# A routed feed-forward stage that gathers its tokens by a slot table and adds into the output rows in place

## The reference

```python
top_w, top_i = jax.lax.top_k(xf @ Wg + bg, 2)
top_w = jax.nn.softmax(top_w, axis=-1)
w_dense = jnp.sum(jax.nn.one_hot(top_i, E) * top_w[..., None], axis=1)
for e in range(E):                       # E = 8, W1 256 x 1024, W2 1024 x 256
    h = jax.nn.gelu(xf @ W1[e] + b1[e], approximate=False)
    out = out + w_dense[:, e:e + 1] * (h @ W2[e] + b2[e])
```

## Time and profile before

| | us |
|---|---|
| median of 3 executions | 6163.82 |
| lowest and highest | 6153.75, 6172.43 |
| the profiled execution | 6173.5 |
| its span, first to last instruction | 6171.7 |
| PE busy | 4328.9 (70%) |
| DVE busy | 3208.3 (52%) |
| ACT busy | 2796.2 (45%) |
| POOL busy | 3500.6 (57%) |

### The profile page before, as it was taken

One profiled execution on the slowest core, in us unless ns is written; L12 is line 12 of the kernel. 1 busy time (PEld: TensorE's weight loads), 2 busy tenths in 40 slices (PEclk: granted clock), 3 DMA queues, 4 the chain that ended last, 5 costly groups with the idle time before them and its releaser, 6 DMA issues. The chain is left out here.

```text
span 6171.7 us, 87850 instructions
## 1 busy us (share of the span) xinstructions
PE 4328.9 (70%) x20635; PEld 3204.3 (52%) x20636; DVE 3208.3 (52%) x8723; ACT 2796.2 (45%) x8562; POOL 3500.6 (57%) x3692
## 2 busy tenths in 40 slices
PE   7388888888888886746666666655555134999990
PEld 4266666666666665534444444444444123666660
DVE  3477767777777776744455554544444421222222
ACT  3367667676766675344444444433333011222220
POOL 0477777777777774067777777777776043000006
PEclk9699989999999998878777778777777557999995
DMA  4688888888888886445555555556664314111105
GB/s 159 182 242 243 242 237 241 238 244 240 242 243 242 242 243 197 141 133 140 141 142 141 141 141 140 136 158 165 166 169 123 127 53 165 35 34 33 33 29 167
DMA packets 700203, 1007.30 MB, mean 163 GB/s; under 512 B 385852, under 2 KB 489369, under 8 KB 699503
## 3 DMA queue, kind: packets, MB, share of 16 engines
q0 software_dynamic: 234384, 745.96, 41.6%
q1 hardware_dynamic: 458450, 249.00, 14.7%
q10 hardware_dynamic: 6924, 7.45, 0.4%
HBM read 904.69 MB, written 90.97 MB: 161 GB/s over the span
## 5 line engine op out<-in xcount | busy, mean ns | idle before, releaser
L806 POOL DMA_INDIRECT walk_ring<-s_h,walk_index x3320 | 3208.3, 966 | 1296.7 <-issue 929.2
L967 PE MATMUL walk_pM<-walk_ring,walk_hit 128*128 128x262 f32 (+1 forms) x9960 | 2769.0, 431 | 11.6 <-ACT walk_ring L831 6.9
L967 PEld LDWEIGHTS walk_pM<-walk_ring,walk_hit 128*128 128x128 f32 x9960 | 2029.4, 212 | 419.1 <-issue 75.1
L831 ACT ACTIVATE walk_ring<-walk_ring 128x128 f32<-128x128 f32 (+1 forms) x6640 | 2134.4, 414 | 5.4
L1197 DVE TENSOR_TENSOR acc<-walk_pM,acc 128x520 f32 (+1 forms) x1494 | 833.8, 558 | 583.3 <-PE walk_pM L967 562.0
L821 ACT ACTIVATE walk_ring<-walk_gap 128x40 f32<-128x40 f32 (+1 forms) x249 | 54.1, 258 | 1915.2 <-DVE walk_gap L1159 1915.2
L871 PE MATMUL walk_pC<-all_ident,walk_best 128*84 128x128 f32 (+1 forms) x166 | 62.3, 375 | 1079.2 <-DVE walk_best L1115 924.1
L871 PEld LDWEIGHTS walk_pC<-all_ident,walk_best 128*84 128x84 f32 (+1 forms) x166 | 20.7, 125 | 1141.7 <-issue 1141.7
L1164 DVE TENSOR_TENSOR walk_hit<-walk_pK,walk_meta 128x512 f32<-128x512 f32 x830 | 561.1, 676 | 12.4 <-PE walk_pM L967 1.0
L1115 DVE TENSOR_TENSOR walk_best<-walk_ring,walk_dt 128x40 f32<-128x40 f32 (+1 forms) x249 | 47.0, 217 | 876.9 <-DMA walk_ring<-s_h,walk_index 876.9
L1851 ACT ACTIVATE expert_hT<-expert_pG,expert_b 128x128 f32<-128x128 f32 x840 | 229.3, 383 | 576.7 <-PE expert_pG L1914 576.5
(11 more groups left out here) (300 smaller groups left out, 3906.4 us busy)
## 6 DMA issues: line engine op xcount, KB each, us to landing
walk_hitT<-s_places SPq DMA_DIRECT2D x166, 640.0 KB
walk_ring<-s_h,walk_index POOLq DMA_INDIRECT x3320
expert_w<-in_fw_dram POOLq DMA_DIRECT2D x16, 1024.0 KB, 7.8
s_xs<-finish_zero POOLq DMA_DIRECT2D x30, 448.0 KB, 18.6
expert_xin<-s_xs SPq DMA_DIRECT2D x105, 128.0 KB, 2.0
s_ys<-expert_out POOLq DMA_DIRECT2D x105, 128.0 KB, 2.0
walk_goal<-walk_target SPq DMA_DIRECT2D x830, 6.0 KB
walk_goal<-walk_target SPq DMA_DIRECT2D x830, 1.5 KB
```

The source lines that it names most:

```text
L806: pool.indirect_dma_start(ring[:, r % RS, t, :], None, table, bass.IndirectOffsetOnAxis(ap=index[:, r % TS, t:t + 1], axis=0)).then_inc(ro ...
L831: last = nc.scalar.activation(row, row, ACT.Copy, scale=ring[:, r % RS, t, at + FH:at + FH + 1])
L967: last = nc.tensor.matmul(pM[:, b, a, 0:WIDE], hit[:, (r * CGROUPS + g) % HBUF, t % GROUP, :], ring[:, r % RS, t, a * HALF_ROW:a * HALF_RO ...
```

## The change

The zero fill of xs goes, with xs, ys and the scratch copy of x1. `finish_layer2` stores x1 straight into the output tensor, and stores y, with the eight gate weights of each token appended to its row (264 columns), into a scratch tensor. Instead of scattering, DVE and PE turn the token-to-slot table round: for each of 98 picks (49 tiles, two choices) DVE builds a mask of the place inside a tile of slots and a mask of the tile, the latter times the token's number plus one, and a matmul of the two adds up in PSUM, so that afterwards column t of partition p holds the token of slot p of tile t, or zero. DVE makes two index tables of it: `token_in` with token 0 for empty slots, `token_out` with a row beyond the end, which a scatter leaves out.

In the expert stage SP loads all weights; POOL gathers the token rows three tiles ahead, gathers the rows of the output (`total`), and scatters them back when DVE has added weight times result. A gather of totals waits until the scatter of the tile before has landed, since a token can be in both. The tile loops are unrolled completely. `combine_pass` goes.

```diff
-        zero = m.sb("zero", [P, SLOTS * D // P // 30])
-        zeros_stored = m.swdge_sem("zeros_stored")
-            @block.gpsimd
-            def _(pool):
-
-                nc.gpsimd.memset(zero[:, :], 0.0)
-                pool.drain()
-                for a in range(30):
-                    w = SLOTS * D // P // 30
-                    pool.dma_start(d["xs"].rearrange("(p s) c -> p (s c)", p=P)[:, a * w:(a + 1) * w], zero[:, :]).then_inc(zeros_stored, 16)
-                pool.wait_ge(zeros_stored, 16 * 30)
...
                 after(sp, x1_ready, NT)
-                sp.dma_start(d["x1"].rearrange("(t p) c -> p t c", p=P), x1[:, :, :]).then_inc(x1_stored, 16)
-                sp.wait_ge(x1_stored, 16)
+                sp.dma_start(d["out"][0:(NT - 1) * P, :].rearrange("(t p) c -> p t c", p=P), x1[:, 0:NT - 1, :]).then_inc(x1_stored, 16)
+                sp.dma_start(d["out"][(NT - 1) * P:N, :], x1[0:LAST, NT - 1, :]).then_inc(x1_stored, 16)
+                after(sp, y_kept, NT)
+                sp.dma_start(d["y"].rearrange("(t p) c -> p t c", p=P)[:, :, 0:D], y[:, :, :]).then_inc(y_stored, 16)
+                sp.wait_ge(gate_ready, 1)
+                sp.dma_start(d["y"].rearrange("(t p) c -> p t c", p=P)[:, :, D:], gate[:, :, :]).then_inc(y_stored, 16)
+                sp.wait_ge(x1_stored, 32)
+                sp.wait_ge(y_stored, 32)
...
-                pool.wait_ge(slots_ready, 1)
-                after(pool, y_kept, NT)
-                for s in range(2):
-                    for t in range(NT):
-                        pool.indirect_dma_start(d["xs"], bass.IndirectOffsetOnAxis(ap=k["slot_out"][:, s, t:t + 1], axis=0),
-                                                y[:, t, :], None, bounds_check=SLOTS - 1, oob_is_err=False).then_inc(scattered, 16)
-                pool.wait_ge(scattered, 16 * 2 * NT)
...
+                for n in range(2 * NT):
+                    pe.wait_ge(picked, n + 1)
+                    last = nc.tensor.matmul(pI[:, 0:TT], place_of[:, n % PICKS, :], token_of[:, n % PICKS, :],
+                                            start=(n == 0), stop=(n == 2 * NT - 1))
+                    last.then_inc(inverted, 1)
...
+                    nc.vector.tensor_tensor(slot[:, s, :], mean[:, :], half[:, :], ALU.add)
+                dve.drain()
+                nc.vector.tensor_copy(slot_i[:, :, :], slot[:, :, :])
+                nc.vector.tensor_tensor(gate[:, :, :], first[:, :, :], spread(k["mix_weight"][:, 0, :], 2, NEXP), ALU.mult)
+                nc.vector.tensor_tensor(code[:, :, :], second[:, :, :], spread(k["mix_weight"][:, 1, :], 2, NEXP), ALU.mult)
+                dve.drain()
...
+                for n in range(2 * NT):
+                    s, t = n % 2, n // 2
+                    if n >= PICKS:
+                        dve.wait_ge(inverted, n - PICKS + 1)
+                    nc.vector.tensor_scalar(place_of[:, n % PICKS, :], k["count"][:, :], slot[:, s, t:t + 1], None, ALU.is_equal)
+                    nc.vector.tensor_scalar(token_of[:, n % PICKS, :], k["count"][:, 0:TT], slot_tile[:, s, t:t + 1], label[:, t:t + 1],
+                                            ALU.is_equal, ALU.mult).then_inc(picked, 1)
...
+                dve.wait_ge(inverted, 2 * NT)
+                nc.vector.tensor_scalar(found[:, :], pI[:, 0:TT], -1.0, None, ALU.add)
+                dve.drain()
+                nc.vector.tensor_scalar(empty[:, :], found[:, :], 0.0, float(OUT_OF_RANGE), ALU.is_lt, ALU.mult)
+                nc.vector.tensor_scalar(token_of[:, 0, :], found[:, :], 0.0, None, ALU.max)
+                dve.drain()
+                nc.vector.tensor_tensor(found[:, :], found[:, :], empty[:, :], ALU.add)
+                nc.vector.tensor_copy(k["token_in"][:, :], token_of[:, 0, :])
+                dve.drain()
+                nc.vector.tensor_copy(k["token_out"][:, :], found[:, :])
...
+    SX = 4
+    SZ = 2
+        xin = m.sb("xin", [P, SX, YROW])
+        total = m.sb("total", [P, SZ, D])
...
-        weights_in = [m.swdge_sem("w1_in"), m.swdge_sem("w2_in")]
+        weights_in = [m.sem(f"weights_in{e}") for e in range(NEXP)]
...
                 sp.dma_start(b1[:, :, :], d["fb1_t"]).then_inc(bias_in, 16)
-                sp.dma_start(b2[:, :, :], d["fb2"].partition_broadcast(P)).then_inc(bias_in, 16)
-
-                def load_tokens(i, j):
-                    t = i * UE + j
-                    sp.wait_ge(x_turned, t + 1)
-                    sp.dma_start(xin[:, j % SX, :], d["xs"][bass.ds(t * P, P), :]).then_inc(x_in[j % SX], 16)
-
-                loop(sp, load_tokens)
+                for e in range(NEXP):
+                    sp.dma_start(w1[:, e, :, :], d["fw1"][e].rearrange("(k p) h -> p k h", p=P)).then_inc(weights_in[e], 16)
+                    sp.dma_start(w2[:, e, :, :], d["fw2"][e].rearrange("(c p) o -> p c o", p=P)).then_inc(weights_in[e], 16)
+                    if e == 0:
+                        sp.dma_start(b2[:, :, :], d["fb2"].partition_broadcast(P)).then_inc(bias_in, 16)
+                for e in range(NEXP):
+                    sp.wait_ge(weights_in[e], 32)
+                    sp.sem_inc(experts_in, 1)
+
+            @block.gpsimd
+            def _(pool):
+                def gather_tokens(t):
+                    if t >= SX:
+                        pool.wait_ge(x_turned, t - SX + 1)
+                        pool.wait_ge(total_ready, t - SX + 1)
+                    pool.indirect_dma_start(xin[:, t % SX, :], None, d["y"],
+                                            bass.IndirectOffsetOnAxis(ap=k["token_in"][:, t:t + 1], axis=0)).then_inc(x_in[t % SX], 16)
+
+                def gather_totals(t):
+                    if t >= 1:
+                        pool.wait_ge(total_stored[(t - 1) % SZ], 16 * ((t - 1) // SZ + 1))
+                    pool.indirect_dma_start(total[:, t % SZ, :], None, d["out"],
+                                            bass.IndirectOffsetOnAxis(ap=k["token_in"][:, t:t + 1], axis=0)).then_inc(total_in[t % SZ], 16)
+
+                def scatter_totals(t):
+                    pool.wait_ge(total_ready, t + 1)
+                    pool.indirect_dma_start(d["out"], bass.IndirectOffsetOnAxis(ap=k["token_out"][:, t:t + 1], axis=0),
+                                            total[:, t % SZ, :], None, bounds_check=N - 1, oob_is_err=False).then_inc(total_stored[t % SZ], 16)
+
+                for t in range(SX - 1):
+                    gather_tokens(t)
+                for t in range(TT):
+                    gather_totals(t)
+                    if t + SX - 1 < TT:
+                        gather_tokens(t + SX - 1)
+                    scatter_totals(t)
+                for j in range(SZ):
+                    pool.wait_ge(total_stored[j], 16 * len(range(j, TT, SZ)))
 
...
+                    if t >= 1:
+                        act.wait_ge(down_done, t)
                     for c in range(HC):
...
+                def take_out(t):
+                    e = dve.value_load(k["expert"][0:1, t:t + 1], min_val=0, max_val=NEXP - 1)
                     dve.wait_ge(down_done, t + 1)
-                    nc.vector.tensor_tensor(out[:, j % SX, :], pO[:, j % RX, 0:D], b2[:, e, :], ALU.add).then_inc(out_ready, 1)
-
...
+                def add_total(t, e):
+                    dve.wait_ge(out_ready, t + 1)
+                    dve.wait_ge(total_in[t % SZ], 16 * (t // SZ + 1))
+                    nc.vector.scalar_tensor_tensor(out=total[:, t % SZ, :], in0=out[:, t % 2, :], scalar=xin[:, t % SX, bass.ds(e + D, 1)],
+                                                   in1=total[:, t % SZ, :], op0=ALU.mult, op1=ALU.add).then_inc(total_ready, 1)
+
+                copy_tokens(0)
+                copy_pre(0)
+                copy_tokens(1)
+                expert = [None] * TT
+                for t in range(TT):
+                    if t + 1 < TT:
+                        copy_pre(t + 1)
+                    if t + 2 < TT:
+                        copy_tokens(t + 2)
+                    if t >= 1:
+                        add_total(t - 1, expert[t - 1])
+                    expert[t] = take_out(t)
+                add_total(TT - 1, expert[TT - 1])
...
+                def down(t, e):
+                    if t >= 2:
+                        pe.wait_ge(out_ready, t - 1)
...
-                for e in range(NEXP):
-                    pool.dma_start(w1[:, e, :, :], d["fw1"][e].rearrange("(k p) h -> p k h", p=P)).then_inc(weights_in[0], 16)
-                    pool.dma_start(w2[:, e, :, :], d["fw2"][e].rearrange("(c p) o -> p c o", p=P)).then_inc(weights_in[1], 16)
-                    pool.wait_ge(weights_in[0], 16 * (e + 1))
-                    pool.wait_ge(weights_in[1], 16 * (e + 1))
-                    pool.sem_inc(experts_in, 1)
...
-                def store_rows(i, j):
-                    t = i * UE + j
-                    pool.wait_ge(out_ready, t + 1 + RX)
```

(23 more changed lines are left out.)

214 lines of the change are left out of this document (76 added, 138 removed).

## The result

The kernel after takes **6074.2 us** (median of 4, 6071.77 to 6075.82) beside 6162.9 for the kernel before on the same chip: ratio 0.9859, interval 0.9848 to 0.9871. That is 89 us less, in the profiled spans 98.5 (6171.7 to 6073.2). The forecast of 5932 had 232 less, and 6074 lies above its range.

What follows compares the result with a forecast made beforehand. The prediction took POOL's issue to pace routing, PE the expert stage, and POOL and DVE the combining stage. Its terms, -13 - 70 + 0 + 0 - 151 + 2 = -232, gave 5932 us against the median, range 5895 to 6030.

Steps and rivals of the forecast that it cites:

- Part 4: Steady expert tiles: three indirect DMAs and a chain of totals of 6.6 to 7.1 us hide under PE's 7.98; cost 0.
- Rival A: Expert tiles: the chain of totals takes 8.75 us, 0.77 over a tile, adding 81 us to reach 6013; chance 0.13.
- Part 3: Start of expert stage: a 13 us stall goes, 13 us lost under SP's weight loads; net 0, from -10 to +20.
- The stall of the first tiles: Start of expert stage: DVE's add waiting for a free row buffer while POOL loads weights; removing it saves 13 us.
- The 13 us for the chain of totals under the weight loads: Start of expert stage: SP's queued 17.8 MB slow the first rounds of scatters and gathers, losing 10 to 16 us.
- Part 2: Routing: 98 scatters give way to mask-and-matmul picks, PE-paced at half clock, 0.51 us each, 50 in all; -70 us.
- rival C: Picks and start: PE reaches full clock in the picks and the start costs little, -11 - 10, 5911; inside forecast's 0.78.
- The row at 0.50: Before the picks, 4950 to 4990: clock at 0.50 with PE busy 34 of 40 us, cited for half-clock picks.
- Part 5: End: the combining stage goes, leaving one add, a hand-over, a scatter and the ending after the last add; -151 us.
- Part 1: First finishing stage: without the zero fill, loads land in about 6 us and DVE waits less; -13 us, between 5 and 20.

Runs made afterwards that it cites:

- run 5: run 4 plus two unread gathers per tile between a scatter's landing and the gather of totals: 6115.6 us, tile period 9.54 us.
- run 9: Kernel after with six token buffers, each expert announced early, totals added before copies, tokens gathered before totals, row p for empty slots: 5914.4 us.
- run 10: run 9 with each later expert's weight loads held until certain tiles' tokens are turned, a probe for this routing only: 5911.2 us.
- run 6: Kernel after with the zero fill's 30 stores put back under finishing stage 1, into a tensor nobody reads: 6083.7 us.
- run 4: Kernel after with six token buffers instead of four, and each expert announced after the next one's loads are issued: 5915.9 us.
- run 2: Kernel after with SP announcing each expert's weights after issuing the next expert's loads, not after all sixteen loads: 6060.4 us.
- run 7: Kernel after with empty slots gathering row p of their own partition instead of row 0: 6078.2 us.
- run 12: Kernel after with 128 extra waits ahead of PE's first tile: 6983.0 us, measured once on a slower chip (kernel before 7078.3).
- run 3: Kernel after, still four token buffers, with DVE adding the previous tile's totals ahead of its two copies: 5937.8 us.

## Why the prediction was wrong

**Part 4, "Cost 0", is the step that failed**, and with it the forecast. It followed one chain, scatter, landing, gather of totals, add, and had its length right: 6.6 to 7.1 forecast, 7.0 found (run 5), hidden in 105 tiles but two. Two of its terms were off and nearly cancel, which is luck: POOL starts 0.83 us behind DVE and not 0.3, and the gather of totals lands in 2.75 and not 3.1. It didn't ask what else stands behind that chain's wait. On POOL the gather of tokens is queued behind the wait for the scatter's landing; on DVE the add that releases the scatter is queued behind the copy that waits for PE's turning of tokens; and four buffers make the gathered tile the one that PE turns next. The three together close a second loop of 8.96 us, +102. The prediction spoke of what stands behind the waiting *add* on DVE, and never of what stands behind the waiting *gather* on POOL. Rival A had the right kind of thing, a chain a little longer than a tile (8.75, 6013), but another chain, which the test that the prediction named (DVE waiting for totals) would not have shown; PE's wait on its tokens does. The late landings that such a loop takes on, 25 us less the 7 that short tiles give back, stood in no term.

**Part 3, net 0, was 28 too low at the start.** The stall of the first tiles went, and was worth 10 us and not 13, since PE made part of it up. But the prediction took SP's queueing of 17.8 MB as free for SP itself. Each issue held it for up to 7.7 us, and the announcement of expert 0 stands behind all sixteen: +28.3. The 13 us for the chain of totals under the weight loads could hardly show here, since PE started when the last of these had been issued. In runs 9 and 10, with slack and early announcement, that loss is 6.1 us. Per transfer the prediction's 3 us more was about right: beside the weight loads scatters and gathers of totals land 3.3 to 3.7 us later (run 9). The loss is smaller than 13 because only two rounds, of 14.2 and 11.4 us, run beside them and the tiles' slack covers a part. The Trainium skill (DMA: Bandwidth & Descriptors, SWDGE vs HWDGE vs iDMA) has the two queues take turns by packets, from which the prediction had estimated 1.5 us per transfer and a loss of 5. The trace doesn't agree with the 1.5, and that the 5 lies near 6.1 is chance.

**Part 2, -70, was -87.8.** The picks were sized as PE-paced at the half clock, 0.51 us each and 50 in all; they are DVE-paced, 0.44 and 43.2. The clock did rise, as rival C had it, but that isn't what made them faster, since they came every 0.44 us at 0.50 already: a pick's two matmuls of 105 columns take no more than 0.44 at the half clock, the low end of the prediction's own 0.43 to 0.52. The rule of the Trainium skill (TensorE: Matmul & The Clock Gate, What's actually happening) that a busy array is let through to the full clock agrees with the trace here: 1.00 from 5000.8 on. The row at 0.50 that I set against it stays unexplained: in those 40 us PE was idle three times, for 1.24 us, and worked without a pause between, and its clock stayed 0.50 all the same. DVE's pace, put at 0.40, is 0.44. The table behind the picks took 4.5 us and the operations ahead of them 0.6 more, 5.1 for 7.6. The remaining 8 us: before, 10.3 us lay between the last scatter's landing and the next stage, now 2.0 lie behind the last cast. No run tests why.

**Part 5, -151, was -136.4**: the end was taken as one add and one scatter behind the last bias add, but the chain of totals has two rounds left there, at 7.8 us with gathers of mostly empty slots that all read row 0. With different rows and slack 8.4 us are left (run 9).

**Part 1, -13, was -10.4**, and +9.7 when put back (run 6). The row loads land in 9.6 us at most, for 23.8, and DVE's waits for rows in that stage went from 23.1 us to 13.3. The wait for parameters fell by 1.6 more (9.1 to 7.5); the prediction had taken a larger part of it.

The gain that the prediction summed up is there once the loop and the start are repaired: run 4 does it with two edits and is at 5915.9, run 9 at 5914.4, where 5932 was forecast. These two are the fastest versions found that hold for any routing, and nothing separates them.

## What to carry to other kernels

When a change adds a wait to an engine's stream, list everything that stands behind the wait on that engine, and follow each of those through its buffer back to the wait: a loop through a ring of buffers has a period of its own, whatever the chain that one was thinking of takes. Prefetches belong ahead of the waits on their queue, and the announcement of the first load ahead of the issue of the last. Leave the loop a microsecond of slack; without it late landings are passed on, and gains elsewhere shrink in it (27 us at the start were worth 14 in run 2, and 28 with slack in run 4).

## What the runs showed of the hardware

- An indirect gather whose indices are nearly all the same row lands in 3.4 to 3.9 us, against 2.8 for 128 different rows. With different rows for the empty slots it is 2.6 to 2.8 (run 7; run 9 too, but for two gathers of tokens at 3.7).
- Issuing a load of 1 MB can hold the issuing engine once several are queued: of sixteen in a row every second took 4.4 to 7.7 us from the fifth on and those between 0.7 to 1.3, against 0.43 for the first.
- Beside such loads an indirect scatter or gather of 128 rows lands in 5.8 to 6.4 us, against 2.5 and 2.75 without them (run 9, the first two scatters and the gather of totals between them).
- An indirect scatter on POOL starts 0.83 us after the end of the DVE add that releases it (5309.62 to 5310.45), and never in under 0.83 in 105 tiles. The plain stores before start 0.65 us after the add in nearly all tiles (store at 5500.43 behind an add that ends near 5499.78); the 0.3 that the prediction carried over the earlier trace rows is that of the last store.
- Packets of PE's code, 16 KB in every third tile of straight-line code, go with tiles that are 0.4 to 0.9 us longer where a loop has no slack (run 12, tiles 46 to 70), and with none that is longer where it has (run 3).
- In a stretch at full clock PE sat idle for 3.28 us, up to 5446.79. Its granted clock was 1.00 up to 5447.9, then 0.50 up to 5451.3, then 1.00 again, and its 16 matmuls of `down` took 5.31 us instead of 3.62 (tile 37).
